# Pacing the slot-list writes of a fused attention and mixture-of-experts kernel: each write waits for the one before it to land, except in the last four sequences

## What is computed

```
x = layernorm(x + attention(x))            # 16 heads of 16 features
gates = softmax(x_flat @ gating_w)         # 4096 tokens, 8 experts
topk_w, topk_idx = top_k(gates, 2)
norm_w = topk_w / (sum(topk_w) + 1e-8)
position = (running count of the items of that expert) - 1
valid = position < 1280                    # capacity of an expert
buf[expert, position] = x_flat[token]      # where valid
h = relu(buf @ w1 + b1);  out_e = h @ w2 + b2
out_flat[token] += out_e[expert, position] * norm_w
x = layernorm(x + out_flat)
```

## Time and profile before

| | |
|---|---|
| device time, median of 3 runs | 820.92 us (819.75 to 821.11) |
| span of the profiled execution | 856.8 us |
| TensorE matmul busy | 784.5 us, 92% |
| VectorE busy | 605.1 us, 71% |
| ScalarE busy | 442.1 us, 52% |
| GpSimd busy | 410.2 us, 48% |
| slot-list writes (line 533) | 64, mean 1023 ns |
| granted TensorE clock, mean | 0.971 |

### The profile page before, as it was taken

One profiled execution on the slowest core, in us unless ns is written; L12 is line 12 of the kernel. 1 busy time (PEld: TensorE's weight loads), 2 busy tenths in 40 slices (PEclk: granted clock), 3 DMA queues, 4 the chain that ended last, 5 costly groups with the idle time before them and its releaser, 6 DMA issues.

```text
span 856.8 us, 16628 instructions
## 1 busy us (share of the span) xinstructions
PE 784.5 (92%) x5919; PEld 648.5 (76%) x5919; DVE 605.1 (71%) x1325; ACT 442.1 (52%) x753; POOL 410.2 (48%) x595
## 2 busy tenths in 40 slices
PE   7699989999989985896999999999999999999994
PEld 7577766677667653585889898898898888988993
DVE  5768878888888885683756856756657568665983
ACT  3166757777666664542534534534345345443670
POOL 1011245555555546457146445254364462556675
PEclk9799999999999998799899999999999999999998
DMA  5677765555555572326145245253352451533741
GB/s 158 135 165 161 161 153 113 114 113 114 116 114 110 115 141 73 116 51 180 20 91 109 41 89 115 43 130 50 81 111 40 96 112 31 140 57 57 288 179 46
DMA packets 71534, 92.75 MB, mean 108 GB/s; under 512 B 12972, under 2 KB 55885, under 8 KB 71324
## 3 DMA queue, kind: packets, MB, share of 16 engines
q1 hardware_dynamic: 53308, 67.95, 31.0%
q0 software_dynamic: 16928, 22.15, 14.9%
q10 hardware_dynamic: 1216, 1.57, 0.8%
HBM read 39.18 MB, written 26.89 MB: 77 GB/s over the span
## 4 chain that ended last, share of the span: by engine, by line
PE 69%; DVE 14%; issue 5%; POOL 3%; another core or an unknown queue 3%; DMA 2%; ACT 2%; ACTq 1%; POOLq 0%; DVEq 0%; SPq 0%
PE bank L1718 14%; DVE negm L890 10%; PE wide L1687 8%; PE wide L1685 8%; PE wide L1686 8%; PE bank L985 7%; PE bank L1720 7%; PE wide L1030 5%; PE bank L1664 2%; PE wide L1048 2%; PE bank L1095 2%; PE bank L1064 1%; PE bank L994 1%; POOL slot_list L533 1%
## 5 line engine op out<-in xcount | busy, mean ns | idle before, releaser
L1359 POOL DMA_INDIRECT acc_rows<-o_w,lists x70 | 120.4, 1720 | 181.6 <-ACT o_w L1508 167.9
L890 DVE TENSOR_REDUCE negm<-wide 128x4 f32<-128x1024 f32 x128 | 156.1, 1222 | 50.5 <-PE wide L1030 31.7
L630 ACT ACTIVATE probs<-wide 128x1024 f32<-128x1024 f32 x128 | 131.0, 1024 | 89.1 <-PE wide L1048 68.9
L1475 ACT ACTIVATE h<-wide,b1T 128x512 f32<-128x512 f32 (+1 forms) x200 | 115.0, 600 | 96.8 <-PE wide L1687 69.1
L1720 PE MATMUL bank<-stack,h_lo 128*128 128x256 f32 x560 | 156.9, 280 | 0.0
L1685 PE MATMUL wide<-g_hi,stack 128*128 128x512 f32 (+1 forms) x400 | 140.8, 352 | 5.2 <-DVE g_lo L1536 4.1
L1687 PE MATMUL wide<-g_hi,stack 128*128 128x512 f32 (+1 forms) x400 | 140.1, 350 | 0.1
L1686 PE MATMUL wide<-g_lo,stack 128*128 128x512 f32 (+1 forms) x400 | 140.1, 350 | 0.0
L1508 ACT ACTIVATE o_w<-o_b,lists 128x256 f32<-128x256 f32 x70 | 35.7, 510 | 148.6 <-DVE o_b L1646 135.5
L1718 PE MATMUL bank<-stack,h_hi 128*128 128x512 f32 x304 | 108.7, 401 | 1.3 <-DVE o_b L1646 1.3
L1720 PEld LDWEIGHTS bank<-stack,h_lo 128*128 128x128 f32 x560 | 105.6, 189 | 0.0
(11 more groups left out here) (211 smaller groups left out, 1640.9 us busy)
## 6 DMA issues: line engine op xcount, KB each, us to landing
stack<-qk SPq DMA_DIRECT2D x180, 128.0 KB, 4.2
w_raw<-in_L_ffn_w SPq DMA_DIRECT2D x16, 1024.0 KB
x_sb<-in_L_attn_x SPq DMA_DIRECT2D x16, 256.0 KB, 5.1
x_rows<-x SPq DMA_DIRECT2D x16, 256.0 KB
acc_rows<-x SPq DMA_DIRECT2D x16, 256.0 KB
acc_sb<-acc_rows SPq DMA_DIRECT2D x8, 512.0 KB, 11.1
out<-acc_sb SPq DMA_DIRECT2D x8, 512.0 KB
x_rows<-zrow SPq DMA_DIRECT2D x2, 1152.0 KB, 6.6
```

What stands on the lines that cost most here:

```text
L630: nc.scalar.activation(probs[:, i % 4].rearrange("p x c t -> p x (c t)"), shifted_banks(i)[:, :, :], ACT.Exp, scale=SCALE).then_inc(exp_do ...
L890: nc.vector.tensor_reduce(negm[n % 2][:, :, :, u].rearrange("p c x -> p x c"), score_banks(PAIRS * n + u)[:, :, :].rearrange("p x (c t) -> ...
L1359: nc.gpsimd.indirect_dma_start(out=acc_d, out_offset=bass.IndirectOffsetOnAxis(ap=lists[:, e, QC * c + r, 0:1], axis=0), in_=o_w[c][:, r, ...
L1475: ins = nc.scalar.activation(h[u % 2][:, t], banks[BZ[u % 4]][:, t], ACT.Relu, bias=b1T[:, FT * e + f:FT * e + f + 1])
```

## The change

In front of each slot-list write GpSimd gets one more wait. For a write (m, c, k) it waits until `listed[m % 4]` shows that the writes before it, of this sequence and of the sequences that share its semaphore, have landed. The last four sequences get none.

```diff
                 pool.wait_ge(token_done, m + 1)
                 pool.wait_ge(weight_done, m + 1)
                 for k in range(TOPK):
+                    if m < LTAIL and (m or c or k):
+                        pool.wait_ge(listed[m % 4], 16 * (QC * TOPK * (m // 4) + TOPK * c + k))
                     nc.gpsimd.indirect_dma_start(
                         out=list_d, out_offset=bass.IndirectOffsetOnAxis(ap=dest[m % 4][:, c, k:k + 1], axis=0),
                         in_=item[m % 4][:, c, k, :], in_offset=None, bounds_check=NE * CAP - 1,
```

## The result

The changed kernel takes 865.27 us (median of 4 runs, 858.1 to 867.69), the kernel before 820.81 us (819.75 to 821.11, 4 runs): a ratio of 1.0528 over all their runs (the quotient of the two medians is 1.054), 95% interval 1.0504 to 1.0552. By the medians that is 44.5 us slower. The forecast had slower as the likeliest sign, by 4.6 us, with a range that ended at 840. So the sign is right and the size is off by a factor of ten.

A forecast was written before the change was run, and what follows sets the result against it. The prediction took GpSimd's chain, about 21.4 us per sequence against a 20.0 us period, to become the first stage's bound; 9.5 + 1.1 - 6 = + 4.6 us gave 825.5 us, range 804 to 840.

The forecast's parts named there:

- the hold-up: TensorE's signals delayed at write bursts, seen as unnamed chain pieces: some 1.4 us per period, 9.16 at 329.99; spacing removes part.
- Who bounds the stage: First stage after the change: GpSimd's chain for one sequence, 21.4 us, exceeds the 20.0 us period and becomes the bound.
- The size of a step: Write start to next write in GpSimd's chain, landing plus 0.52 us to go on: 3.69 first, then 4.2 and 4.2.
- The rule of the Trainium skill: GpSimd-issued transfers have a fixed cost of about 2.0 us: step 2.5, chain 16.9 us, so the kernel would get faster.
- Its own sign for the hold-up: If the unnamed 1.3 us chain pieces stay although the writes are spaced, the burst isn't what makes them.
- Sequences 1 to 8: First-stage periods, each followed by a later sequence's xT_hi: 8 x 1.4 = 11.2 us longer.
- Sequence 0: First write to next xT_hi: 13.10 us available, 13.1 needed, so nothing lost or won.
- The end: Last sequences of the first stage: + 1.1 us at sequence 9, nothing at 10, - 6 as the 9.16 us mostly goes.
- The slack of 1.75 us: Between xT_lo's end and TensorE's queries: the first 1.75 us of GpSimd's delay reach nobody, taken off once.
- The landings are short: Rival: writes land in 3.17 us or less everywhere and spacing wins, faster, put at 811 us; chance 0.38.
- the two cancel: Rival: GpSimd's chain between 20.6 and 21.0 us, waits and regained hold-up balance, 821 us; chance 0.12.
- The far slower one: Rival: landings of 4.2 us, 849, or hold-ups absent in runs without a profile, 846; chance 0.10.

The follow-up runs named there:

- Experiments 5: Changed kernel with all 36 waits, third write of sequences 0 to 10 moved behind the next layer-norm factors, fourth behind the next entries: 832.69 us, ratio 1.0164.
- 7: Changed kernel with each of the 36 waits replaced by GpSimd clearing a small buffer eight times, no landing waited for: 869.99 us, ratio 1.0603.
- 8: Changed kernel with waits in sequences 0 to 8 alone, third and fourth writes of sequences 0 to 10 moved behind later GpSimd work: 823.06 us, ratio 1.0047.
- second profile: The kernel before, unedited, timed and profiled once more with the experiments: 820.71 us, ratio 0.9999, profiled span 820.1 us.

## Why the prediction was right about the bound and wrong about the hold-up

**Who bounds the stage: right.** The prediction made GpSimd's chain the bound of the period, 8.26 us + three steps + 1.05, at 21.4 us. The mean of the eight periods is 21.65, the idle time in front of `xT_hi` is gone, and the waits behind `xT_lo` and `shift` are there. Experiments 5, 7 and 8 show that it is this chain: other work of the same length costs the same, and the same waits cost nearly nothing where the chain stays under 18.6.

**The size of a step: right, within 0.16 us in the mean.** It took 3.69 + 4.2 + 4.2 = 12.1 us for three; they are 12.56 in the mean (3.63, 3.94 and 4.99). Part of that is luck: the landings were a little shorter than forecast and GpSimd went on later, 0.7 us or more after a landing where 0.52 was taken. Single landings are spread further than the bounds of 3.17 and 4.2 us: from 2.11 to 6.39. Two rows of the chain, one of either end, both on writes made after the change:

```profile
226.46 2.11 DMA slot_list<-item,dest
...
334.06 6.39 DMA slot_list<-item,dest
```

The rule of the Trainium skill that was weighed against it (a fixed 2.0 us; page "DMA: Bandwidth & Descriptors", section "Anatomy of one DMA - SWDGE (gpsimd) path") is near the shortest that occurs, 2.11 us. Its estimate of 16.9 us for the chain doesn't agree with the 21.65 measured.

**"I take it as real": the step that failed.** The sum went against a period of 20.0 us and credited the spacing with a hold-up of 1.3 to 1.4 us per period and 9.16 at the end. The second profile of the kernel before has neither. The prediction itself named the sign, runs that are 36 us shorter than the profiled one, and put what follows from it into a rival of 0.10. Its own sign for the hold-up couldn't tell: the unnamed pieces are gone in the changed kernel as it said, but they are gone in the second profile of the kernel before as well. This one assumption is behind the largest parts of three terms:

- Sequences 1 to 8: 8 x 1.4 = 11.2 was forecast, 24.0 measured. Of that 12.8, 8 x 1.35 = 10.8 is the period of 18.65 for 20.0, and 2.0 is the step.
- Sequence 0: nothing was forecast, since 13.10 us lay between its first write and the next `xT_hi`. In the second profile there are 8.8 (110.49 to 119.28), and after the change 15.3 (111.46 to 126.80), with steps of 4.5, 4.9 and 5.0 us: + 6.5. Of that, 4.3 is the room that was not there (8.8 for 13.1) and 2.2 the longer steps.
- The end: 1.1 for sequence 9, less 6, was forecast, + 10.7 measured. There was no 9.16 to win back, so a later GpSimd is a loss without anything against it. From sequence 9's first write to the next layer norm (`veps`) it is 11.5 us for 10.7, from sequence 10's 16.3 for 11.3, and from sequence 11's 17.8 for 11.1; 2.0 us are made up behind it. Sequence 10 is a mistake of its own: the prediction put it at nothing, and it is + 5.0, with two steps of 5.05 and 7.15 us. In the second profile GpSimd has 6.33 us of idle time in front of `veps` in sequence 10, but none in sequence 11, whose four writes are followed by the four of sequence 12. That GpSimd is the one that others wait for there was forecast; that there is no gain to set against it was not.

**The slack of 1.75 us** once didn't show: the delay goes from GpSimd's chain to its own next step up to the last list write, and never has to pass through TensorE's slack. The differences from the forecast together: 12.8 + 6.5 + 1.75 + 15.6 (from - 4.9 to + 10.7), and 1.6 at both ends of the table, are 38.2 us, and with the forecast's 4.6 the 42.8 between the spans.

**The rivals.** "The landings are short" (811) and "the two cancel" (821) both lived on the hold-up: without it nothing can be won by spacing, and they would have had no chance. The far slower one had the right reason for 846, a period from 18.6 to 21.4 in 9 sequences, 25 us. What it still missed is the end, 10.7 us, the rest of sequence 0, 3.7, 1.6 in the eight periods (24.0 for 22.4), and the 1.6 at both ends of the table.

## What to carry to other kernels

Before the sum, hold the profiled span against the timed median. If the span is several per cent longer, the pieces of the chain that have no name are the first suspects, and both ends of every term have to be worked out with and without them; here that decided between 4.6 us and the 25 that the prediction worked out without them, of 44.5 measured. A wait on an engine that is half idle is priced per period: its whole chain with the waits, less the period of the engine that sets the pace, and nothing until the slack is used up (3, 10 and 44 us for one, two and three waits, the first two mostly in the one place without slack). Where such a wait can't be avoided, put the engine's other work of the next step between the write and the wait: that took 29.1 us down to 2.2.

## What the runs showed of the hardware

The same kernel, profiled twice, had spans of 856.8 and 820.1 us, with hold-ups of 1.3 to 9.16 us behind bursts of small indirect writes in the first alone, and in none of the ten other profiles. Two more unnamed pieces, of 0.48 and 1.40 us near 404 us of the first, lie behind all list writes. What made them is open.

A small indirect write by GpSimd (8 bytes from each partition) took 2.1 to 6.4 us from its start to its landing in the changed kernel, and it took longer with more traffic beside it. Some stretches from a write's start to its landing in the changed kernel (us, busy time of PE, PEld, DVE, ACT and POOL with instructions, granted clock, share of the DMA engines, GB/s):

```profile
208.70:213.30 4.60, 4.52 (x51) 3.45 (x50) 3.84 (x15) 3.38 (x8) 0.93 (x1) 1.00 1.11 153
223.40:225.70 2.30, 2.30 (x22) 2.08 (x20) 1.92 (x5) 1.80 (x4) 1.10 (x1) 1.00 0.01 0
...
229.40:233.60 4.20, 4.02 (x50) 3.05 (x49) 3.87 (x10) 2.66 (x4) 0.96 (x1) 1.00 0.45 132
334.10:340.40 6.30, 4.40 (x54) 3.00 (x50) 6.09 (x21) 3.81 (x5) 0.92 (x1) 1.00 0.88 304
```

At a share of 0.01 it landed in 2.3 us, at 0.45 in 4.2, at 1.11 in 4.7, and at 0.88 with 304 GB/s, beside two loads of 1 MB of weights issued 3 us before, in 6.4. Over the 34 landings that the chain of this profile shows, 18 had a share of 0.21 or less and took 2.1 to 3.7 us, 2.8 in the mean; 16 had 0.43 or more and took 2.8 to 6.4 us, 4.2 in the mean. The two groups overlap, so the share doesn't set the time of a single write, and no run changed the traffic alone. I had expected 3.2 to 4.2 us everywhere.
